# Where the stores of the first 63 rows stand in the queues, and how the last two row groups are cut into pieces

## The chip, the cores and the metric

The kernel runs on one core of one Trainium2 chip. The metric is the device time of one execution in microseconds (us), as the median of several runs. The profile is of one execution more, and times inside it are counted from the start of its span.

## What is computed

```python
N, D = (8192, 64)                      # x: 8192x64, adj: 8192x8192, u: 8192x64, all float32
keep = (u >= 0.1).astype(x.dtype)
x_drop = x * keep / (1.0 - 0.1)
y = x + jnp.matmul(adj, x_drop)        # adj has few nonzeros but is stored dense: 268 MB
m = jnp.mean(y, axis=-1, keepdims=True)
v = jnp.var(y, axis=-1, keepdims=True)
return (y - m) / jnp.sqrt(v + 1e-5)
```

The host part of the kernel reorders adj into blocks, so that every transfer reads one contiguous stretch of memory. Nothing is computed there.

## The kernel before, in words

The 8192 rows of the output are 64 rows on each of the 128 partitions (`KT` = 64). A "row" below is one of these 64, so 128 rows of the output. For each row, the products run over 64 tiles of adj with 128x128 elements (64 KB each), one for each value of t. The weights are the 64 columns of x_drop for t, the moving operand is the adj tile, and even and odd t go to the lower and the upper half of the partitions of the accumulator (line 203). The result is transposed and in two halves. A copy of it to `acc_sb` (line 253, `take`) and a product with `twofold`, a stacked identity matrix (line 210, `turn_back`), turn it back and add the halves. VectorE then adds x, takes mean and variance of each row and normalises it (`normalise`, lines 256 to 288), with ScalarE's square root in between (line 178). The normalised rows overwrite x in SBUF (`normed` is `x_nat`).

Rows come in groups. Twelve groups of 5 rows (`FULL`, `R`) run in loops; their adj comes in three slots of 24, 24 and 16 tiles into a ring that holds exactly one group. Then follow two small groups that are written out: 3 rows (rows 60 to 62), and the last row (63). `TAIL` lists the pieces in which their adj is loaded, in tiles. In the 3-row group a tile is three 128x128 blocks wide (192 KB), and in the last row it is one (64 KB). In the text, T0.0 to T0.4 are the pieces of the 3-row group and T1.0, T1.1, ... those of the last row.

Queues and their order:

- SyncE (SP) issues x and u and all of adj in one queue (q1 in the profile). Before each load it waits until TensorE has used the part of the ring that the load overwrites (lines 154 and 160).
- ScalarE (ACT) issues the three stores in a second queue (q10). The store of the first 60 rows (line 186, 1920 KB) goes out when the twelfth group is normalised, the store of rows 60 to 62 (line 191, 96 KB) when the 3-row group is, and that of the last row (line 196, 32 KB) at the end. Then ACT waits until all three have landed.
- TensorE (PE) takes the pieces in order (lines 227 to 246). After the first piece of the last row it turns back the 3-row group and adds x of the last row to `final` (line 241).
- The last three tiles of the last row (`DIRECT` = 2 pieces) are multiplied the other way round, straight into `final` (line 235), so that the copy of the accumulator and its product with `twofold` (line 246) run before the last tile is there.
- VectorE ends with the statistics of `final`, the reciprocal and the normalisation (lines 310 to 316).

Of the kernel before, what the change touches and what calls it, by code (L numbers as in the profile page):

```python
# [6 lines left out]
D = 64  # L7
P = 128
KT = N // P
# [6 lines left out]
R = 5  # L16
FULL = 12
TILE = R * P
# [3 lines left out]
MAIN = FULL * SLOTS  # L22
# [3 lines left out]
COLS = TILE // 2  # L26
SPLIT = TILE // COLS

TAIL = [(3, [26, 15, 11, 8, 4]), (1, [13, 16, 12, 8, 6, 4, 2, 2, 1])]
LAST = len(TAIL) - 1  # L30
FIRST_ROW = [FULL * R + sum(rows for rows, _ in TAIL[:n]) for n in range(len(TAIL))]
FIRST_PIECE = [sum(len(tiles) for _, tiles in TAIL[:n]) for n in range(len(TAIL))]

DIRECT = 2
HALVED = KT - sum(TAIL[LAST][1][-DIRECT:])
X_PARTS = 4
PART = KT * D // X_PARTS
PT = KT // X_PARTS

assert FULL * R + sum(rows for rows, _ in TAIL) == KT  # L40
assert all(sum(tiles) == KT for _, tiles in TAIL) and sum(SLOT_TILES) == KT

# [12 lines left out]
def build(nc: bass.Bass, xu: bass.AP, adj: bass.AP, out: bass.AP):  # L55
# [6 lines left out]
    out_rows = out.rearrange("(p t) d -> p (t d)", p=P)  # L62
# [6 lines left out]
    def tail_block(start, width):  # L69
        first = (FULL * RING + start) * P  # L70
        return adj[first:first + width * P].rearrange("(p c) -> p c", p=P)

    with ExitStack() as ctx:
        def sb(name, shape):
            return ctx.enter_context(nc.sbuf_tensor(name, shape, fp32))

        def sem(name):
            return ctx.enter_context(nc.semaphore(name))

        def ps(name, cols):  # L80
            return ctx.enter_context(nc.psum_tensor(name, [P, cols], fp32))

        adj_ring = sb("adj_ring", [P, RING])
# [4 lines left out]
        x_drop = x_and_u[:, KT * D:2 * KT * D]  # L88

        normed = x_nat  # L90
        identity = sb("identity", [P, P])
        twofold = sb("twofold", [P, D])
        eps = sb("eps", [P, 1])
        acc_sb = sb("acc_sb", [P, TILE])
# [12 lines left out]
        acc = [ps(f"acc{b}", 512) for b in range(SPLIT)]  # L107
        tail_acc = [ps(f"tail_acc{n}", 512) for n in range(len(TAIL))]
        back = ps("back", 512)
        final = ps("final", 512)  # L110
# [6 lines left out]
        adj_used = sem("adj_used")  # L117
# [2 lines left out]
        zeros_ready = sem("zeros_ready")  # L120
        identity_ready = sem("identity_ready")
        twofold_ready = sem("twofold_ready")
        halved_ready = sem("halved_ready")
        acc_copied = sem("acc_copied")
        back_ready = sem("back_ready")
        sum_ready = sem("sum_ready")
# [6 lines left out]
        std_ready = sem("std_ready")  # L133
        rstd_ready = sem("rstd_ready")
        normed_ready = sem("normed_ready")
        final_stats = sem("final_stats")
        final_var = sem("final_var")
        out_stored = sem("out_stored")
# [4 lines left out]
        def _(sp):  # L143
# [12 lines left out]
            for n in range(len(TAIL)):  # L156
                for i, (_, _, at, width) in enumerate(pieces(n)):
# [2 lines left out]
                    sp.wait_ge(adj_used, MAIN - SLOTS + slot)  # L160
                    sp.dma_start(adj_ring[:, at:at + width], tail_block(at, width)).then_inc(piece_loaded[n][i], 16)  # L161

        @block.gpsimd
        def _(pool):
            nc.gpsimd.memset(eps[:], EPS).then_inc(eps_ready, 1)  # L165
            nc.gpsimd.memset(identity[:], 0.0).then_inc(zeros_ready, 1)
            pool.wait_ge(zeros_ready, 1)
            nc.gpsimd.affine_select(out=identity[:], in_=identity[:], compare_op=ALU.not_equal, fill=1.0,
                                    base=0, pattern=[[-1, P]], channel_multiplier=1).then_inc(identity_ready, 1)

            pool.wait_ge(identity_ready, 1)
            nc.gpsimd.tensor_tensor(twofold[:], identity[:, 0:D], identity[:, D:P], ALU.add).then_inc(twofold_ready, 1)

        @block.scalar
        def _(act):
            def root(n, rows):
                act.wait_ge(squares_ready, n + 1)
                nc.scalar.activation(std[:, 0:rows], squares[:, 0:rows], ACT.Sqrt, scale=1.0 / D,  # L178
                                     bias=eps[:]).then_inc(std_ready, 1)

            act.wait_ge(eps_ready, 1)
            with act.Fori(0, FULL) as g:
                root(g, R)
            act.wait_ge(normed_ready, FULL)
            cols = slice(0, FULL * R * D)
            act.dma_start(out_rows[:, cols], normed[:, cols]).then_inc(out_stored, 16)
            for n in range(LAST):
                root(FULL + n, TAIL[n][0])
            act.wait_ge(normed_ready, FULL + LAST)
            cols = slice(FULL * R * D, (KT - 1) * D)  # L190
            act.dma_start(out_rows[:, cols], normed[:, cols]).then_inc(out_stored, 16)
            act.wait_ge(final_var, 1)
            nc.scalar.activation(std[:, 0:1], mean_var[:, 1:2], ACT.Sqrt, bias=eps[:]).then_inc(std_ready, 1)  # L193
            act.wait_ge(normed_ready, FULL + LAST + 1)
            cols = slice((KT - 1) * D, KT * D)
            act.dma_start(out_rows[:, cols], normed[:, cols]).then_inc(out_stored, 16)
            act.wait_ge(out_stored, 16 * 3)

        @block.tensor
        def _(pe):  # L200
            def product(into, cols, at, t, end):
                h = t % 2
                return nc.tensor.matmul(into[h * D:(h + 1) * D, 0:cols], x_drop[:, t * D:(t + 1) * D],  # L203
                                        adj_ring[:, at:at + cols], start=(t < 2), stop=(t >= end - 2))

            def turn_back(rows, done):

                pe.wait_ge(acc_copied, done + 1)
                for r in range(rows):
                    last = nc.tensor.matmul(back[:, r * D:(r + 1) * D], acc_sb[:, r * P:(r + 1) * P], twofold[:],  # L210
                                            start=True, stop=True)
                last.then_inc(back_ready, 1)

            pe.wait_ge(twofold_ready, 1)
            with pe.Fori(0, FULL) as g:
                for s in range(SLOTS):
                    pe.wait_ge(chunk_loaded[s], (g + 1) * 16)
                    for pair in range(SLOT_FIRST[s], SLOT_FIRST[s] + SLOT_TILES[s], 2):
                        if pair % PT == 0:
                            pe.wait_ge(drop_ready, pair // PT + 1)  # L220
                        for b in range(SPLIT):
                            for t in (pair, pair + 1):
                                last = product(acc[b], COLS, t * TILE + b * COLS, t, KT)
                    last.then_inc(adj_used, 1)
                turn_back(R, g)

            for n, (rows, _) in enumerate(TAIL):
                for i, (before, count, at, _) in enumerate(pieces(n)):
                    pe.wait_ge(piece_loaded[n][i], 16)
                    for t in range(before, before + count):  # L230
                        col = at + (t - before) * rows * P
                        if n < LAST or t < HALVED:
                            last = product(tail_acc[n], rows * P, col, t, KT if n < LAST else HALVED)
                        else:
                            last = nc.tensor.matmul(final[:, 0:D], adj_ring[:, col:col + P],  # L235
                                                    x_drop[:, t * D:(t + 1) * D], start=False, stop=(t == KT - 1))
                    last.then_inc(adj_used, 1)
                    if n == LAST and i == 0:

                        turn_back(TAIL[n - 1][0], FULL + n - 1)  # L240
                        nc.tensor.matmul(final[:, 0:D], identity[:], x_nat[:, (KT - 1) * D:KT * D],  # L241
                                         start=True, stop=False)
                    if n == LAST and i == len(TAIL[n][1]) - 2:

                        pe.wait_ge(acc_copied, FULL + LAST + 1)
                        nc.tensor.matmul(final[:, 0:D], acc_sb[:, 0:P], twofold[:], start=False, stop=False)  # L246

        @block.vector
        def _(dve):
            def take(into, cols, used):  # L250
                dve.wait_ge(adj_used, used)
                for b, part in enumerate(into):
                    last = nc.vector.tensor_copy(acc_sb[:, b * cols:(b + 1) * cols], part[:, 0:cols])  # L253
                last.then_inc(acc_copied, 1)
# [36 lines left out]
            for i in range(X_PARTS):  # L291
                cols = slice(i * PART, (i + 1) * PART)
# [9 lines left out]
            for n in range(LAST):  # L302
                rows = TAIL[n][0]
                take([tail_acc[n]], rows * P, MAIN + FIRST_PIECE[n] + len(TAIL[n][1]))
                normalise(FULL + n, FIRST_ROW[n], rows)

            take([tail_acc[LAST]], P, MAIN + FIRST_PIECE[LAST] + len(TAIL[LAST][1]) - DIRECT)

            dve.wait_ge(adj_used, MAIN + FIRST_PIECE[LAST] + len(TAIL[LAST][1]))
            nc.vector.bn_stats(stats[:, 0, :], final[:, 0:D]).then_inc(final_stats, 1)  # L310
            dve.wait_ge(final_stats, 1)
            nc.vector.bn_aggr(mean_var[:], stats[:, 0, :]).then_inc(final_var, 1)  # L312
# [38 lines left out]
```

## Time and profile before

| | us |
|---|---|
| median of 3 runs (lowest, highest) | 645.89 (645.62, 645.92) |
| the profiled execution | 645.73 |
| its span, first to last instruction | 643.8 |
| PE busy | 512.4 (80%) |
| DVE busy | 60.8 (9%) |
| ACT busy | 19.6 (3%) |
| data moved | 274.80 MB, mean 427 GB/s |

The strip of the 16 DMA engines shows 9 (90% or more) in every one of its 40 slices but the last. PE idles 114.1 us in the main loop, always for adj. In the page, busy time of PE is modelled, since matmuls overlap; PEld is its weight load. "DMA to landing" is the time from the issue of a transfer to the arrival of its semaphore. MB and GB count 1000s, KB in the list of DMA issues counts 1024s.

### The profile page before, as it was taken

To read this page: it belongs to the slowest core of one execution; us is meant where nothing else is said; L and a number is where in the kernel's file an instruction comes from. 1 tells how busy PE (TensorE), PEld (TensorE's weight loads), DVE (VectorE), ACT (ScalarE), POOL (GpSimd) and SP (SyncE) were. 2 spreads that over 40 slices of the span, in tenths; PEclk is the share of its full clock that TensorE was granted. 3 is DMA by queue.
4 is the path that set the end of the run, shared out by engine and by line. 5 is a ranking of instruction groups with operands and counts; after the bars stand their busy time and mean duration, and the time that the engine had idled before them with its cause. 6 is when DMAs were issued, how large, how long until landed. Compare 5 with 4: busy or idle time off the path is not lost.

```text
span 643.8 us, 7619 instructions
## 1 busy us (share of the span) xinstructions
PE 512.4 (80%) x3458; PEld 265.4 (41%) x3458; DVE 60.8 (9%) x268; ACT 19.6 (3%) x26; POOL 1.1 (0%) x8
## 2 busy tenths in 40 slices
PE   0088798698798698798698798798798887888987
PEld 0044344344344344444344444444443443444436
DVE  1200200200200200100200200200200110110202
ACT  0000000000000000000000000000000000000000
POOL 0000000000000000000000000000000000000000
PEclk9997988988988987989878988988987987979999
DMA  9999999999999999999999999999999999999996
GB/s 383 428 429 444 432 428 440 428 435 440 428 431 444 428 428 448 428 428 448 428 428 448 428 428 448 428 428 448 428 428 448 428 428 448 428 428 408 421 427 253
DMA packets 7780, 274.80 MB, mean 427 GB/s; under 512 B 992, under 2 KB 1504, under 8 KB 2272
## 3 DMA queue, kind: packets, MB, share of 16 engines
q1 hardware_dynamic: 7344, 272.63, 98.2%
q10 hardware_dynamic: 432, 2.10, 0.8%
q8 instruction: 4, 0.07, 0.0%
HBM read 272.63 MB, written 2.10 MB: 427 GB/s over the span
## 4 chain that ended last, share of the span: by engine, by line
DMA 69%; PE 30%; SPq 0%; issue 0%; DVE 0%; ACT 0%
DMA adj_ring<-adj_blocks 69%; PE acc L203 28%; PE tail_acc L203 2%; SPq L146 0%; PE final L235 0%; PE back L210 0%; SPq L161 0%; SPq L148 0%; DVE x_and_u L316 0%; PE final L246 0%; ACT std L193 0%; DVE stats L310 0%; PE final L241 0%; DVE mean_var L312 0%; DVE rstd L314 0%
## 5 line engine op out<-in xcount | busy, mean ns | idle before, releaser
L203 PE MATMUL acc<-adj_ring,x_and_u 128*64 128x320 f32 x3072 | 465.4, 468 | 114.1 <-DMA adj_ring<-adj_blocks 114.1
L203 PEld LDWEIGHTS acc<-adj_ring,x_and_u 128*64 128x64 f32 x3072 | 233.2, 149 | 341.0 <-DMA adj_ring<-adj_blocks 122.3
L253 DVE COPY acc_sb<-acc 128x320 f32<-128x320 f32 x24 | 10.7, 486 | 517.4 <-PE acc L203 517.4
L203 PE MATMUL tail_acc<-adj_ring,x_and_u 128*64 128x384 f32 (+1 forms) x250 | 29.0, 384 | 2.2 <-DMA adj_ring<-adj_blocks 2.1
L210 PE MATMUL back<-twofold,acc_sb 128*128 128x64 f32 x126 | 16.8, 280 | 11.9 <-DVE acc_sb L253 11.9
L210 PEld LDWEIGHTS back<-twofold,acc_sb 128*128 128x128 f32 x126 | 15.0, 191 | 18.8 <-DVE acc_sb L253 18.7
L178 ACT ACTIVATE std<-squares,eps 128x5 f32<-128x5 f32 (+1 forms) x13 | 3.9, 300 | 615.1 <-DVE squares L278 615.1
L203 PEld LDWEIGHTS tail_acc<-adj_ring,x_and_u 128*64 128x64 f32 x250 | 15.9, 137 | 14.9 <-issue 10.8
L178 ACT ACT_TABLE_LOAD x12 | 15.4, 1283 | 1.2 <-POOL eps L165 1.0
L284 DVE TENSOR_SCALAR x_and_u<-summed,mean,rstd 128x64 f32 (+1 forms) x63 | 15.2, 309 | 0.5
L262 DVE BATCH_NORM_STATS2 stats<-summed 128x6 f32<-128x64 f32 x63 | 9.3, 213 | 0.4
L258 DVE TENSOR_TENSOR summed<-back,x_and_u 128x320 f32<-128x320 f32 (+1 forms) x13 | 6.3, 482 | 20.3 <-PE back L210 20.3
L293 DVE SCALAR_TENSOR_TENSOR x_and_u<-x_and_u 128x1024 f32<-128x1024 f32 x4 | 4.9, 1220 | 12.9 <-DMA x_and_u<-xu 12.9
L253 DVE COPY acc_sb<-tail_acc 128x384 f32<-128x384 f32 (+1 forms) x2 | 0.9, 426 | 23.1 <-PE tail_acc L203 23.1
L281 DVE RECIPROCAL rstd<-std 128x5 f32<-128x5 f32 (+1 forms) x13 | 2.5, 190 | 4.8 <-ACT std L178 4.8
L297 DVE TENSOR_SCALAR x_and_u<-x_and_u 128x1024 f32<-128x1024 f32 x4 | 2.8, 693 | 0.1
L276 DVE TENSOR_SCALAR mean<-twice_mean 128x5 f32<-128x5 f32 (+1 forms) x13 | 2.2, 172 | 0.0
L268 DVE TENSOR_TENSOR gap<-stats 128x5 f32<-128x5 f32 (+1 forms) x13 | 2.2, 169 | 0.5
L269 DVE TENSOR_TENSOR within<-stats 128x5 f32<-128x5 f32 (+1 forms) x13 | 2.1, 160 | 0.0
L270 DVE TENSOR_TENSOR twice_mean<-stats 128x5 f32<-128x5 f32 (+1 forms) x13 | 2.1, 160 | 0.0
L278 DVE TENSOR_TENSOR squares<-within,between 128x5 f32<-128x5 f32 (+1 forms) x13 | 2.1, 160 | 0.0
L272 DVE SCALAR_TENSOR_TENSOR between<-gap 128x5 f32<-128x5 f32 (+1 forms) x13 | 2.0, 157 | 0.0
(19 smaller groups left out, 5.8 us busy)
## 6 DMA issues: line engine op xcount, KB each, us to landing
adj_ring<-adj_blocks SPq DMA_DIRECT2D x24, 7680.0 KB, 33.3
adj_ring<-adj_blocks SPq DMA_DIRECT2D x12, 5120.0 KB, 36.9
adj_ring<-adj_blocks SPq DMA_DIRECT2D x1, 4992.0 KB, 26.0
x_and_u<-xu SPq DMA_DIRECT2D x1, 4096.0 KB, 12.1
adj_ring<-adj_blocks SPq DMA_DIRECT2D x1, 2880.0 KB, 17.6
adj_ring<-adj_blocks SPq DMA_DIRECT2D x1, 2112.0 KB, 26.2
out<-x_and_u ACTq DMA_DIRECT2D x1, 1920.0 KB, 13.8
adj_ring<-adj_blocks SPq DMA_DIRECT2D x1, 1536.0 KB, 29.9
```

Source lines behind the costliest of these rows:

```text
L178: nc.scalar.activation(std[:, 0:rows], squares[:, 0:rows], ACT.Sqrt, scale=1.0 / D, bias=eps[:]).then_inc(std_ready, 1)
L203: return nc.tensor.matmul(into[h * D:(h + 1) * D, 0:cols], x_drop[:, t * D:(t + 1) * D], adj_ring[:, at:at + cols], start=(t < 2), stop=(t ...
L210: last = nc.tensor.matmul(back[:, r * D:(r + 1) * D], acc_sb[:, r * P:(r + 1) * P], twofold[:], start=True, stop=True)
L253: last = nc.vector.tensor_copy(acc_sb[:, b * cols:(b + 1) * cols], part[:, 0:cols])
L258: nc.vector.tensor_tensor(summed[:, 0:rows * D], back[:, 0:rows * D], x_nat[:, bass.ds(row * D, rows * D)], ALU.add).then_inc(sum_ready, 1)
L262: last = nc.vector.bn_stats(stats[:, r, :], summed[:, r * D:(r + 1) * D])
L268: nc.vector.tensor_tensor(gap[:, 0:rows], m0, m1, ALU.subtract).then_inc(gap_ready, 1)
L276: nc.vector.tensor_scalar(mean[:, 0:rows], twice_mean[:, 0:rows], 0.5, None, ALU.mult)
L281: nc.vector.reciprocal(rstd[:, 0:rows], std[:, 0:rows]).then_inc(rstd_ready, 1)
L284: last = nc.vector.tensor_scalar(normed[:, bass.ds((row + r) * D, D)], summed[:, r * D:(r + 1) * D], mean[:, r:r + 1], rstd[:, r:r + 1], A ...
L293: nc.vector.scalar_tensor_tensor(out=x_drop[:, cols], in0=x_drop[:, cols], scalar=P_DROP, in1=x_nat[:, cols], op0=ALU.is_ge, op1=ALU.mult) ...
L297: nc.vector.tensor_scalar(x_drop[:, cols], x_drop[:, cols], 1.0 / (1.0 - P_DROP), None, ALU.mult).then_inc(drop_ready, 1)
```

## The change

The stores of the first 60 rows and of rows 60 to 62 are no longer issued by ScalarE in q10 but by SyncE in q1, behind the last piece of adj. Each waits there for the same semaphore as before. The store of the last row stays with ScalarE. The pieces of the 3-row group become 24, 16, 10, 8 and 6 tiles (they were 26, 15, 11, 8 and 4), and those of the last row 20, 18, 14, 8 and 4 (they were 13, 16, 12, 8, 6, 4, 2, 2 and 1). All 64 tiles of the last row go through the transposed accumulator, so that its copy and the product with `twofold` come after the last tile. That product now raises a semaphore, `final_ready`, on which VectorE waits.

```diff
-TAIL = [(3, [26, 15, 11, 8, 4]), (1, [13, 16, 12, 8, 6, 4, 2, 2, 1])]
+TAIL = [(3, [24, 16, 10, 8, 6]), (1, [20, 18, 14, 8, 4])]
...
-DIRECT = 2
-HALVED = KT - sum(TAIL[LAST][1][-DIRECT:])
...
                     sp.dma_start(adj_ring[:, at:at + width], tail_block(at, width)).then_inc(piece_loaded[n][i], 16)
+
+            sp.wait_ge(normed_ready, FULL)
+            cols = slice(0, FULL * R * D)
+            sp.dma_start(out_rows[:, cols], normed[:, cols]).then_inc(out_stored, 16)
+            sp.wait_ge(normed_ready, FULL + LAST)
+            cols = slice(FULL * R * D, (KT - 1) * D)
+            sp.dma_start(out_rows[:, cols], normed[:, cols]).then_inc(out_stored, 16)
...
             with act.Fori(0, FULL) as g:
                 root(g, R)
-            act.wait_ge(normed_ready, FULL)
-            cols = slice(0, FULL * R * D)
-            act.dma_start(out_rows[:, cols], normed[:, cols]).then_inc(out_stored, 16)
             for n in range(LAST):
                 root(FULL + n, TAIL[n][0])
-            act.wait_ge(normed_ready, FULL + LAST)
-            cols = slice(FULL * R * D, (KT - 1) * D)
-            act.dma_start(out_rows[:, cols], normed[:, cols]).then_inc(out_stored, 16)
...
-                        if n < LAST or t < HALVED:
-                            last = product(tail_acc[n], rows * P, col, t, KT if n < LAST else HALVED)
-                        else:
-                            last = nc.tensor.matmul(final[:, 0:D], adj_ring[:, col:col + P],
-                                                    x_drop[:, t * D:(t + 1) * D], start=False, stop=(t == KT - 1))
+                        last = product(tail_acc[n], rows * P, col, t)
...
-                    if n == LAST and i == len(TAIL[n][1]) - 2:
-
-                        pe.wait_ge(acc_copied, FULL + LAST + 1)
-                        nc.tensor.matmul(final[:, 0:D], acc_sb[:, 0:P], twofold[:], start=False, stop=False)
+            pe.wait_ge(acc_copied, FULL + LAST + 1)
+            nc.tensor.matmul(final[:, 0:D], acc_sb[:, 0:P], twofold[:], start=False, stop=True).then_inc(final_ready, 1)
...
-            take([tail_acc[LAST]], P, MAIN + FIRST_PIECE[LAST] + len(TAIL[LAST][1]) - DIRECT)
-
-            dve.wait_ge(adj_used, MAIN + FIRST_PIECE[LAST] + len(TAIL[LAST][1]))
+            take([tail_acc[LAST]], P, MAIN + FIRST_PIECE[LAST] + len(TAIL[LAST][1]))
+            dve.wait_ge(final_ready, 1)
```

## Rows read from the trace of the kernel before

**Rows 1.** Page, part 3: the stores' queue, packets, MB, share of 16 engines.

```profile
q10 hardware_dynamic: 432, 2.10, 0.8%
```

**Rows 2.** Busy time of each engine by stretch; last columns PEclk, DMA share, GB/s.

```profile
583.30:605.00 21.70, 21.70 (x160) 11.37 (x160) 0.00 (x0) 0.00 (x0) 0.00 (x0) 1.00 0.99 429
611.00:625.00 14.00, 11.94 (x74) 5.05 (x72) 0.19 (x1) 0.00 (x0) 0.00 (x0) 1.00 0.97 414
637.00:638.00 1.00, 1.00 (x22) 1.00 (x20) 0.00 (x0) 0.00 (x0) 0.00 (x0) 1.00 0.60 194
638.00:639.00 1.00, 1.00 (x24) 1.00 (x22) 0.00 (x0) 0.00 (x0) 0.00 (x0) 1.00 0.24 70
```

**Rows 3.** Chain that ended last, in order of time: start us, us, what.

```profile
627.28 5.67 PE tail_acc L203 x50
...
633.99 5.39 PE tail_acc L203 x96
```

**Rows 4.** Timeline of PE's weight loads: start us, us, what, [idle before <-releaser].

```profile
606.01 1.19 PEld L210 LDWEIGHTS back<-twofold,acc_sb 128*128 128x128 f32 x10 [1.55 <-DVE acc_sb L253]
...
607.65 0.14 PEld L203 LDWEIGHTS tail_acc<-adj_ring,x_and_u 128*64 128x64 f32 x2 [0.18 <-issue]
...
620.22 0.14 PEld L203 LDWEIGHTS tail_acc<-adj_ring,x_and_u 128*64 128x64 f32 x1 [0.19 <-issue]
623.08 0.20 PEld L203 LDWEIGHTS tail_acc<-adj_ring,x_and_u 128*64 128x64 f32 x4 [2.72 <-DMA adj_ring<-adj_blocks]
...
631.21 0.85 PEld L203 LDWEIGHTS tail_acc<-adj_ring,x_and_u 128*64 128x64 f32 x16 [0.50 <-DMA adj_ring<-adj_blocks]
```

**Rows 5.** Page, part 6: DMA issues, count, KB each, us from issue to landing.

```profile
out<-x_and_u ACTq DMA_DIRECT2D x1, 1920.0 KB, 13.8
...
adj_ring<-adj_blocks SPq DMA_DIRECT2D x1, 832.0 KB, 32.9
adj_ring<-adj_blocks SPq DMA_DIRECT2D x1, 512.0 KB, 31.8
...
out<-x_and_u ACTq DMA_DIRECT2D x1, 96.0 KB, 2.9
adj_ring<-adj_blocks SPq DMA_DIRECT2D x1, 64.0 KB, 13.7
out<-x_and_u ACTq DMA_DIRECT2D x1, 32.0 KB, 1.5
```

**Rows 6.** Timeline of SP's queue: issues of T1.0, T1.3 and T1.8.

```profile
598.26 0.43 SPq L161 DMA_DIRECT2D adj_ring<-adj_blocks  x1
...
605.06 0.33 SPq L161 DMA_DIRECT2D adj_ring<-adj_blocks  x1
...
625.61 1.68 SPq L161 DMA_DIRECT2D adj_ring<-adj_blocks  x1
```

**Rows 7.** Timeline of all engines, from the first store's issue to the last's.

```profile
611.22 0.38 ACTq L186 DMA_DIRECT2D out<-x_and_u  x1
...
631.42 0.56 DVE L253 COPY acc_sb<-tail_acc 128x384 f32<-128x384 f32 x1 [20.23 <-PE tail_acc L203]
...
632.88 0.88 PE L210 MATMUL back<-twofold,acc_sb 128*128 128x64 f32 x6
...
633.92 5.46 PE L203 MATMUL tail_acc<-adj_ring,x_and_u 128*64 128x128 f32 x96
...
636.65 0.34 ACTq L191 DMA_DIRECT2D out<-x_and_u  x1
...
639.50 0.29 DVE L253 COPY acc_sb<-tail_acc 128x128 f32<-128x128 f32 x1 [2.88 <-PE tail_acc L203]
639.85 0.43 PE L246 MATMUL final<-twofold,acc_sb 128*128 128x64 f32 x2
...
640.54 0.23 DVE L310 BATCH_NORM_STATS2 stats<-final 128x6 f32<-128x64 f32 x1 [0.75 <-PE final L235]
...
641.93 0.34 ACTq L196 DMA_DIRECT2D out<-x_and_u  x1
```

More of the change, by code:

```diff
@@ L122, in build @@
         twofold_ready = sem("twofold_ready")
-        halved_ready = sem("halved_ready")
         acc_copied = sem("acc_copied")
@@ L135, in build @@
         normed_ready = sem("normed_ready")
+        final_ready = sem("final_ready")
         final_stats = sem("final_stats")
@@ L200, in _, with product @@
         def _(pe):
-            def product(into, cols, at, t, end):
+            def product(into, cols, at, t):
                 h = t % 2
                 return nc.tensor.matmul(into[h * D:(h + 1) * D, 0:cols], x_drop[:, t * D:(t + 1) * D],
-                                        adj_ring[:, at:at + cols], start=(t < 2), stop=(t >= end - 2))
+                                        adj_ring[:, at:at + cols], start=(t < 2), stop=(t >= KT - 2))
             def turn_back(rows, done):
@@ L222, in _ @@
                             for t in (pair, pair + 1):
-                                last = product(acc[b], COLS, t * TILE + b * COLS, t, KT)
+                                last = product(acc[b], COLS, t * TILE + b * COLS, t)
                     last.then_inc(adj_used, 1)
```

## Prediction, made before the changed kernel was run

> **What bounds the kernel now.** I read the strips of the page first, then the busy time by stretch, then PE's weight loads and the landings of the pieces over the last 40 us. The strip of the DMA engines is full to the last slice, and in a stretch with loads alone they move 429 GB/s at a share of 0.99 [rows 2]. So the time is that of the bytes, plus what comes after the last byte of adj, plus whatever else stands in the queue before that byte. The stores do stand there: q10 moves 2.10 MB [rows 1], of which 1.97 MB (1920 KB) go out at 611.22, while adj is still being loaded [rows 5, 7].
>
> The last 40 us need a closer look, because there the bound changes hands. From 606.01 on PE works off the turning back of the twelfth group and then the pieces of the 3-row group [rows 4]. It keeps up a pace of one 3-row tile per (620.22 - 607.65) / 39 = 0.322 us, while a tile of 192 KB (0.197 MB) takes the DMA engines 0.197 / 0.429 = 0.458 us. PE has a stock, though: T0.0 and T0.1 are there when it starts on them. It runs without a wait for 41 tiles. Then its weight loads stand 2.72 us until T0.2 has landed (623.08), waits again before T0.3, and once more, 0.50 us, before T1.0 at 631.21 [rows 4]. The chain that ended last shows the rest as PE alone: from 627.28 to the end of the products at 639.38, in two long blocks [rows 3]. So the end of this kernel is set by both: the pieces land only just ahead of PE. Landings are issue plus time to landing [rows 5, 6]: T1.0 at 598.26 + 32.9 = 631.2, T1.3 at 605.06 + 31.8 = 636.9, T1.8 at 625.61 + 13.7 = 639.3.
>
> **Stores behind the loads.** While the store of 1920 KB was in flight (611.22 to 625.0) all queues together moved 414 GB/s, a little under the 429 of loads alone [rows 2]. So the loads lost what the store took. Without it, each piece that lands after 625 lands 1.966 / 0.427 = 4.6 us earlier (by 0.414 it would be 4.75; I take the smaller). The store of 96 KB is worth 0.2 us, of the last tiles only.
>
> The wait that moves to SP costs nothing: behind it in SP's queue stand only the two stores. The first one's condition is met at 611.2, the second one's as long after the 3-row group is turned back as before, 636.65 - (632.88 + 0.88) = 2.9 us [rows 7], which is 634.2 by the times below, while the first store is still running. Their price is the time after the loads. The DMA engines do the same bytes in all, in another order, and none of them idles before the end, so q1 should run dry when the loads and stores of before did. The load share ends around 637.3 (0.60 in 637 to 638), with a few slow engines on until 639.0 (0.24) [rows 2], and the store of 96 KB landed at 636.65 + 2.9 = 639.55 [rows 5, 7]. I take 639.6 for the two moved stores. Loads alone then end around 637.3 - 4.6 = 632.7, with stragglers to 634.7.
>
> No row shows a store running with no load beside it. Its cost is bounded from below by the joint rate (4.6 us for 1.966 MB, the row for which the engines were 97% busy), and from above by its own pace beside the loads, 13.8 us [rows 5]. I take 4.6, because the joint rate hardly fell while it ran: it looks like sharing, and not like a limit of the store.
>
> The Trainium skill (DMA: Bandwidth & Descriptors, Specifications) gives a core about 358 GB/s of HBM. The loads here run at 429 [rows 2], so the trace does not agree for reads; for writes alone no row shows it. By that figure the two stores would take 5.8 us where I have 4.8, and would land an estimated 1 us later, at 640.6.
>
> **New pieces of the 3-row group.** The same 64 tiles. T0.0 (24 tiles, 2 fewer) lands before 607.2, but PE is not free sooner: its weight loads for turning back end at 606.01 + 1.19 = 607.20 [rows 4]. So PE starts where it did. Is it then ever short of data? 40 tiles keep it busy to about 620.2. T0.2 (50 tiles) lands about 618.2: the 41st tile was there at 614.05, and 9 more take 4.1 us. T0.4 lands about 624.6 (T1.0's landing below, less 20 small tiles of 0.0655 MB / 0.427 = 0.153 us each), and PE wants it after 58 tiles, at 626.0. So PE runs through, and 24 tiles after 620.22 it starts T1.0, at 620.22 + 24 x 0.322 = **627.96**, where it was 631.21. That is 3.25 us. PE is now the bound: the other 1.4 us of the 4.6 are not on its path.
>
> T1.0 must be there by then. It has 20 tiles now. 13 landed at 631.2 and 49 (through T1.3) at 636.9, 0.158 us a tile, so 20 would have at 632.3, and 4.6 earlier that is 627.7. The margin is only 0.3 us, and this is the weakest link of the sum. If it fails, the rest shifts by what is missing.
>
> **New pieces of the last row.** Before, the products up to the turning back took 632.88 - 631.21 = 1.67 us for 13 tiles, and 48 tiles took 5.46, or 0.114 each [rows 4, 7]. Seven more before the turning back: it starts at 627.96 + 1.67 + 0.80 = 630.43. The copy that it needs (0.56 us, right after the last 3-row product [rows 7]) has 2.4 us of cover. Turning back and adding x take 633.92 - 632.88 = 1.04: 631.47. Then 44 tiles at 0.114 take 5.01: the products end at **636.48**, against 639.38. The pieces land by the same reckoning (interpolated, less 4.6) at 630.5 (T1.1, wanted 631.5), 632.8 (T1.2, 633.5), 634.1 (T1.3, 635.1) and 634.7 (T1.4, 636.0), each 0.7 to 1.3 us ahead. Four transfers fewer save nothing on the path. A piece fewer means a coarser wait, which costs nothing as long as PE is behind the data.
>
> **Last row without direct products.** Three tiles move from one form to the other at the same price (they are in the 44). Copy and product with `twofold` came beside the direct products, and now stand alone on the path. The copy starts 0.12 us after the last product, as before (639.38 to 639.50), takes 0.29, then 0.06, then 0.43 for the product [rows 7]. VectorE's statistics start at 636.48 + 0.12 + 0.29 + 0.06 + 0.43 + 0.02 = 637.40, against 640.54 [rows 7]. So this way of ending takes 0.92 us from the last transposed product to the statistics, where the old took 1.16 with its three direct tiles.
>
> **Sum.** Everything after that is unchanged: the last store is issued at 641.93 - 3.14 = 638.79 and lands 1.5 us later, at 640.3, against 643.4. The moved stores (639.6) have landed by then, with 0.7 us to spare. Span 643.8 - 3.14 = 640.66, and the profiled execution 645.73 - 3.14 = 642.6. The median of the runs lies 0.16 above the profiled execution, so I forecast **642.7**.
>
> **Rivals.**
>
> *Data still last* (PE waits at T1.0 or later). For it: the margin of 0.3 us, and slow engines that finish up to 2 us behind the mean, which decide when a piece counts as landed. Against: removing the store takes the same off every engine. If the pieces come 0.3 to 1 us later than I reckon, the time is 643.0 to 643.5. Chance 0.13.
>
> *Stores last, but not badly.* The two stores run at some 300 GB/s with nothing beside them: 6.9 us instead of 4.8, landing at 641.7 instead of 640.3 for the last row's, span 642.1, time 644.1. For it: reading SBUF and writing HBM with all engines is not in the trace. At 358 GB/s it would be 642.9 to 643.0. Chance 0.09.
>
> *Stores last, and slower than before.* The 13.8 us were the store's own limit, 1.966 MB at 142 GB/s, and not its share. It would then start at 632.7 and land at 646.5: span 646.9, time 648.8, 2.9 us slower. It decides from a length of 643.4 - 632.7 = 10.7 us, or 184 GB/s. Against it: beside the store the total would then have had room to be the full 429 and was 414, and the loads gave way to it. Chance 0.06.
>
> *The stores do not wait behind the loads.* If SP's queue let the store's packets in among the loads, the landings would be as before, PE's gaps would stay, and the end would differ only by the shape of the last row: 645.5 to 646.2. Against: pieces of one queue landed in the order of their issue. Chance 0.05. I count here too whatever gives back the gain without my seeing it.
>
> **How the numbers follow.** The forecast (642.3 to 643.0) has 0.67, the four rivals 0.13, 0.09, 0.06 and 0.05. Range for 8 in 10: from 642.1 (the forecast, less a spread like that of the three runs) to 644.0, which takes in late pieces and most of the milder stores. A measurement of this kernel can tell about 0.2%, 1.3 us, from no change. So faster means under 644.6: 0.67 + 0.13 + 0.09 and a little of the rest, less something for an unseen loss, 0.87. Same 0.06, slower 0.07.
>
> **What would show it.** In the profile of the changed kernel: weight loads of PE from 607.3 to about 630 with no wait for adj_ring in them; T1.0's first near 628.0; the statistics of `final` near 637.4; the last store issued near 638.8; and the stores from SP landing by 640. A wait of PE for adj_ring before T1.0 would mean that the data is still last. A share of the DMA engines near 1 but well under 420 GB/s after 633, or a last landing from SP's queue after 640.5, would mean that the stores are. If T1.0 is taken up at 631 as before, the stores were not behind the loads, and the whole sum is wrong.

## The result, and the profile after

The changed kernel takes 644.43 us (median) against 645.75 for the kernel before, in runs of the same session: a ratio of 0.998, with a 95% interval of 0.9973 to 0.9986. So it is faster by about 0.2%, where 0.5% was forecast (642.7 us), and the time lies above the range (642.1 to 644.0). What no part of the prediction speaks of is the spread. The executions of before all lie within 0.6 us (645.53 to 646.14). Those of the changed kernel fall into three groups: 2 at 642.4 and 642.5, 10 between 643.9 and 644.6, and 7 between 645.2 and 645.6. The twentieth, in a slow state of the chip, took 868.78 us at a mean granted clock of 0.57, and says nothing about the change.

The profiled execution took 644.05 us with a span of 642.2: 1.7 less than before, and 1.5 more than forecast. Busy time by stretch, of the changed kernel (last columns PEclk, DMA share, GB/s), as in [rows 2]:

```profile
583.30:605.00 21.70, 21.70 (x150) 11.40 (x152) 0.00 (x0) 0.00 (x0) 0.00 (x0) 0.92 0.99 427
611.00:625.00 14.00, 14.00 (x90) 6.24 (x88) 1.47 (x8) 0.30 (x1) 0.00 (x0) 1.00 1.00 419
...
637.00:638.00 1.00, 0.99 (x20) 0.75 (x14) 0.00 (x0) 0.00 (x0) 0.00 (x0) 1.00 0.33 121
638.00:639.00 1.00, 0.43 (x2) 0.30 (x2) 0.36 (x2) 0.00 (x0) 0.00 (x0) 1.00 0.17 55
```

The first line is the one to look at. PE is busy for the whole stretch in both kernels, but with a granted clock of 0.92 here and 1.00 in [rows 2], and its matmul records are 150 instead of 160. Slices of 1 us show where that is:

```profile
583.00:584.00 1.00, 0.73 (x6) 0.48 (x8) 0.00 (x0) 0.00 (x0) 0.00 (x0) 1.00 0.66 287
584.00:585.00 1.00, 1.00 (x10) 0.53 (x6) 0.00 (x0) 0.00 (x0) 0.00 (x0) 0.81 0.85 369
585.00:586.00 1.00, 1.00 (x6) 0.48 (x4) 0.00 (x0) 0.00 (x0) 0.00 (x0) 0.50 1.52 655
586.00:587.00 1.00, 1.00 (x6) 0.42 (x5) 0.00 (x0) 0.00 (x0) 0.00 (x0) 0.50 0.38 164
587.00:588.00 1.00, 1.00 (x8) 0.42 (x6) 0.00 (x0) 0.00 (x0) 0.00 (x0) 0.50 1.14 492
588.00:589.00 1.00, 1.00 (x10) 0.54 (x8) 0.00 (x0) 0.00 (x0) 0.00 (x0) 0.99 1.52 655
```

For some 3.4 us, from about 584.6 on, the clock is at 0.50 (1.2 instead of 2.4 GHz). PE has then been at work again for 1.3 us, after a wait of 2.13 us. Over this stretch the changed kernel (first line) has 16 matmul records where the kernel before (second line) has 28, while the transfers are the same in both:

```profile
584.60:588.00 3.40, 3.40 (x16) 1.57 (x14) 0.00 (x0) 0.00 (x0) 0.00 (x0) 0.50 0.89 386
584.60:588.00 3.40, 3.40 (x28) 1.83 (x26) 0.00 (x0) 0.00 (x0) 0.00 (x0) 1.00 0.89 386
```

The timeline of PE shows what that does to the last 5-row group, and what came before it:

```profile
565.12 16.01 PE L201 MATMUL acc<-adj_ring,x_and_u 128*64 128x320 f32 x96 [3.54 <-DMA adj_ring<-adj_blocks]
583.26 23.44 PE L201 MATMUL acc<-adj_ring,x_and_u 128*64 128x320 f32 x160 [2.13 <-DMA adj_ring<-adj_blocks]
607.70 1.33 PE L208 MATMUL back<-twofold,acc_sb 128*128 128x64 f32 x10 [0.99 <-DVE acc_sb L245]
```

The same view of the kernel before has the second and third lines as:

```profile
583.27 21.75 PE L203 MATMUL acc<-adj_ring,x_and_u 128*64 128x320 f32 x160 [2.10 <-DMA adj_ring<-adj_blocks]
606.01 1.33 PE L210 MATMUL back<-twofold,acc_sb 128*128 128x64 f32 x10 [0.99 <-DVE acc_sb L253]
```

The block of the last two slots starts at the same moment and takes 23.44 us instead of 21.75. Everything behind it is 1.69 us late. The chain that ended last is PE from there to the end (start us, us, what), where [rows 3] begins only at 627.28:

```profile
594.87 11.87 PE acc L201 x88
...
607.70 1.33 PE back L208 x10
609.03 22.97 PE tail_acc L201 x168
632.00 0.81 PE back L208 x6
632.81 0.22 PE final L235 x2
633.04 4.98 PE tail_acc L201 x88
...
638.11 0.30 DVE acc_sb L245
...
638.46 0.45 PE final L238 x2
...
638.93 0.24 DVE stats L301
```

No wait for adj_ring stands in it. The stores, from the page's list of issues and from the timeline (they answer to [rows 5, 7]):

```profile
out<-x_and_u SPq DMA_DIRECT2D x1, 1920.0 KB, 24.8
...
out<-x_and_u SPq DMA_DIRECT2D x1, 96.0 KB, 3.7
out<-x_and_u ACTq DMA_DIRECT2D x1, 32.0 KB, 1.5
```

```profile
612.90 0.34 SPq L162 DMA_DIRECT2D out<-x_and_u  x1
...
635.70 0.34 SPq L165 DMA_DIRECT2D out<-x_and_u  x1
...
640.31 0.37 ACTq L194 DMA_DIRECT2D out<-x_and_u  x1
```

Issue plus time to landing puts them at 637.7 (612.90 + 24.8), 639.4 (635.70 + 3.7) and 641.8 (640.31 + 1.5), so the last row's store is the last.

### The profile page after: what moved, and what is told of

The parts are those of the page before. It is cut to its first block, busy times and chain, and to the rows that moved or that the text cites. A ratio compares the mean times of both kernels' runs of the same rounds, so it can differ in the third digit from the quotient of the medians.

```text
span 642.2 us, 7615 instructions
## 1 busy us (share of the span) xinstructions
PE 511.6 (80%) x3458; PEld 264.7 (41%) x3458; DVE 60.7 (9%) x268; ACT 19.6 (3%) x26; POOL 1.1 (0%) x8
## 4 chain that ended last, share of the span: by engine, by line
DMA 64%; PE 34%; DVE 0%; issue 0%; SPq 0%; ACT 0%; DVEq 0%
DMA adj_ring<-adj_blocks 64%; PE acc L201 29%; PE tail_acc L201 4%; PE back L208 0%; DVE acc_sb L245 0%; SPq L143 0%; PE final L238 0%; SPq L145 0%; DVE x_and_u L307 0%; ACT std L191 0%; DVE stats L301 0%; PE final L235 0%; DVE mean_var L303 0%; DVE rstd L305 0%; DVEq L243 0%
## 6 DMA issues: line engine op xcount, KB each, us to landing
out<-x_and_u SPq DMA_DIRECT2D x1, 1920.0 KB, 24.8
```

## The experiments

**Theory A:** after the change PE sets the end from the second slot of the last 5-row group on (583.3), with no wait for data behind that. What PE loses to a granted clock of 0.50 there stands in the time, and it differs from execution to execution. Before, PE waited for T0.2, T0.3 and T1.0 [rows 4], and these waits took up the loss. **Theory B:** the spread comes from the transfers, whose landings vary with the stores behind them.

### The stores alone

```diff
 # the kernel before, with
+            sp.wait_ge(normed_ready, FULL)              # the two stores behind the last piece, in SP's queue
+            ...
-            act.wait_ge(normed_ready, FULL)             # and gone from ScalarE
-            ...
```

> The kernel before with only the two stores moved to SyncE's queue behind the last piece; pieces and direct products as before. Theory A (the end is set by PE from the last 5-row group on, so half-clock stretches of PE there show in the time): PE starts the last row near 628.0, statistics of final near 637.3 where no such stretch falls, so 642.5 at best, and otherwise that plus 1.7 us for each half-clock stretch: single executions spread over 642.4 to 645.5, median about 644. Theory B (the transfers' landings vary): here nine small pieces instead of five stand in front of the stores, so the spread should be other than that of the changed kernel, and PE should show waits for adj_ring.

Measured: 644.24 us (643.87 to 645.35, 10 executions), ratio 0.9979 (0.997 to 0.9988). That is the changed kernel's time within the spread of both, so the stores are what moved it. Its profiled execution is one of the late ones, 645.32 us:

```profile
583.30:589.30 6.00, 5.94 (x24) 2.72 (x26) 0.00 (x0) 0.00 (x0) 0.00 (x0) 0.51 1.01 437
589.30:605.00 15.70, 15.70 (x120) 8.22 (x118) 0.00 (x0) 0.00 (x0) 0.00 (x0) 1.00 0.97 418
```

```profile
583.36 24.62 PE L204 MATMUL acc<-adj_ring,x_and_u 128*64 128x320 f32 x160 [3.30 <-DMA adj_ring<-adj_blocks]
...
610.23 22.38 PE L204 MATMUL tail_acc<-adj_ring,x_and_u 128*64 128x384 f32 x154
```

Here the half-clock stretch lasts for the first 6 us of the block, which takes 24.62 us: 2.87 more than 21.75. 645.32 - 2.87 = 642.45, the fastest group. The 3-row products run on without a wait. None of its 10 executions was as fast as that group, which the expectation had allowed for.

### The pieces and the ending alone

```diff
 # the changed kernel, with
-            sp.wait_ge(normed_ready, FULL)              # the two stores gone from SP's queue
-            ...
+            act.wait_ge(normed_ready, FULL)             # and back in ScalarE's, as before
+            ...
```

> The changed kernel with the two stores back in ScalarE's queue. Theory A: the store takes 4.6 us from the loads again, T1.0 (20 tiles) lands near 632.3, PE waits for it, and the end comes at 632.3 + 2.25 + 1.04 + 5.0 + 0.92 = 641.5 for the statistics of final, against 640.54 before: 646.7, and nearly the same in all executions (within 0.6 us), since PE waits for data after any half-clock stretch of the last 5-row group. Theory B: the spread of 3 us stays, since the pieces are those of the changed kernel.

Measured: 646.90 us (646.62 to 647.03, 10 executions), ratio 1.0017 (1.0008 to 1.0026). The spread is gone with the stores, and the time came where the interpolation of landings put it. The profile (646.78 us) has a half-clock stretch too, and waits for data behind it:

```profile
583.32 23.21 PE L200 MATMUL acc<-adj_ring,x_and_u 128*64 128x320 f32 x160 [3.02 <-DMA adj_ring<-adj_blocks]
...
626.49 4.94 PE L200 MATMUL tail_acc<-adj_ring,x_and_u 128*64 128x384 f32 x28 [1.35 <-DMA adj_ring<-adj_blocks]
632.36 2.40 PE L200 MATMUL tail_acc<-adj_ring,x_and_u 128*64 128x128 f32 x40 [0.93 <-DMA adj_ring<-adj_blocks]
```

1.5 us were lost in the block (23.21 - 21.75), and PE waits for data behind it, so they do not set the time. The chain of this profile goes through T1.0, from its issue to its landing (start us, us):

```profile
599.28 33.02 DMA adj_ring<-adj_blocks
```

T1.0, now 20 tiles, lands at 632.3, as expected, where the 13 tiles of before landed at 631.2. That is 1.1 us, about what this kernel is slower by; the piece and the new ending were not changed one at a time.

### The changed kernel again

> The changed kernel itself, for its spread on this chip and another profile. Theory A: executions in groups near 642.4, 644.1 and 645.4; the profile shows in its last 60 us as much PE time at half clock as its time is over 642.4 (1.7 us for each 3.4 us at half clock in which PE was busy). Theory B: the profile shows a late landing, and no clock below 1.00 after 583.

Measured: 644.15 us (642.53 to 645.23, 9 executions: one at 642.5, five at 643.9 to 644.2, three at 645.1 to 645.2), ratio 0.9976 (0.9966 to 0.9986). The profiled one, 644.15 us, has its half-clock stretch in the same place, a block of 23.45 us, and PE turns back the twelfth group at 607.69.

### PE's idle time filled

```diff
+            def dummy(count):
+                for _ in range(count):
+                    nc.tensor.matmul(final[0:D, 0:512], twofold[:], x_drop[:, 0:512], start=True, stop=True)
+
+            pe.wait_ge(drop_ready, 1)
             with pe.Fori(0, FULL) as g:
+                dummy(12)
                 for s in range(SLOTS):
...
                     last.then_inc(adj_used, 1)
+                    if s == 0:
+                        dummy(9)
```

> The changed kernel with idle time of PE in the main loop filled by products that nobody reads (12 of 512 columns before the wait for the first slot, 9 before that for the second, about 5 and 4 us at full clock). Theory A: the granted clock stays 1.00 in the last groups, PE starts the 3-row group at 607.3 or a little before, and all executions lie at 642.3 to 642.9. Theory B: the time spreads over 642.4 to 645.6 as before.

Measured: 717.01 us, ratio 1.1107 (1.1092 to 1.1122). A miss, by a size of my own: one of these products takes 0.85 us and not 0.43, so they overran the idle time and made PE the bound of the main loop. The clock did stay at 1.00 (mean 0.998). With 6 and 5 of them in place of 12 and 9:

> The changed kernel with PE's idle time in the main loop filled less than in the first try: 6 products of 512 columns before the wait for the first slot and 5 before that for the second, 0.85 us each by the first try's trace, so 5.1 and 4.3 us out of 6.8 and 5.4 that are idle when PE runs at full clock. Theory A (PE sets the end, and half-clock stretches after the wait for the second slot of the last 5-row group make the spread): no granted clock under 1.00 after the first groups, the block of products that starts near 583.3 takes 21.7 us, all executions at 642.3 to 642.9. Theory B (landings vary): the spread of 3 us stays.

Measured: **642.51 us** (642.31 to 642.64, 5 executions), ratio 0.995 (0.9935 to 0.9964). The spread of 3 us is gone, and the time is the fastest group's. PE does more work than in the changed kernel, and the kernel is 1.6 to 1.9 us faster (644.15 and 644.43 in its two rounds of runs). The profile (642.31 us):

```profile
583.21 21.75 PE L201 MATMUL acc<-adj_ring,x_and_u 128*64 128x320 f32 x160 [0.71 <-DMA adj_ring<-adj_blocks]
605.96 1.33 PE L208 MATMUL back<-twofold,acc_sb 128*128 128x64 f32 x10 [0.99 <-DVE acc_sb L253]
607.21 23.04 PE L201 MATMUL tail_acc<-adj_ring,x_and_u 128*64 128x384 f32 x168
630.19 0.88 PE L208 MATMUL back<-twofold,acc_sb 128*128 128x64 f32 x6
```

The granted clock is 1.00 over 583.3 to 640. The stores, the pieces and their queues are those of the changed kernel, so this run speaks against Theory B by itself. T1.0's weight loads begin a little late here:

```profile
627.70 1.43 PEld L201 LDWEIGHTS tail_acc<-adj_ring,x_and_u 128*64 128x64 f32 x23 [0.30 <-DMA adj_ring<-adj_blocks]
```

Between other pairs of weight loads the pause is 0.18 us [rows 4], so T1.0 landed about 0.1 us after PE could have used it.

### Only the idle time before the second slot, or only that before the first

In the first variant `dummy(2)` stands behind slot 0 and nothing before it; in the second, `dummy(6)` stands before slot 0 and nothing behind it.

> The changed kernel with PE's idle time filled only before the wait for the second slot (2 products of 512 columns, 1.7 us of some 2.1 to 3.3). Theory A, in its narrow form: it is the idle time right before the second slot of the last 5-row group that brings the half-clock stretch which costs time. Then the block that starts near 583.3 takes 21.7 us and all executions lie at 642.3 to 642.9, although the clock still falls after each wait for the first slot (mean granted clock near 0.93 to 0.95). If the stretches come from anything else, the spread stays.

Measured: 642.51 us (642.34 to 642.52, 5 executions), ratio 0.9949 (0.9936 to 0.9963). The clock still falls elsewhere (mean 0.928), which costs nothing. So filling the idle time right before the second slot is enough. It was filled in all twelve groups, and not tried in the last one only.

> The changed kernel with PE's idle time filled only before the wait for the first slot (6 products). The first slot then runs at full clock and is done near 578, 3 us sooner, so PE idles 5.2 us before the second slot instead of 2 to 3. Theory A: the half-clock stretch after it comes in every execution and costs at least as much as in the changed kernel: 643.7 to 645.7, none near 642.4, median about 645. A theory by which more PE work in the loop simply keeps the whole kernel at full clock would have 642.5.

Measured: 644.06 us (642.37 to 645.89, 7 executions), ratio 0.9975 (0.9961 to 0.999). The spread stays, as Theory A has it, and more PE work alone does not remove it. But the expectation that none would be near 642.4 was wrong: three are at 642.4 to 642.7. The profiled one (642.72 us) is among these, and its line shows a longer wait than the changed kernel's, with no loss behind it:

```profile
583.61 21.75 PE L201 MATMUL acc<-adj_ring,x_and_u 128*64 128x320 f32 x160 [3.44 <-DMA adj_ring<-adj_blocks]
```

The test is less clean than it was meant to be. The six products overran the idle time, from 561.89 to 567.09, while the first slot was there at about 565.1 (565.12 in the changed kernel's timeline). So the first slot ran at full clock but was done at 580.17 and not near 578, and PE idled 3.44 us and not 5.2. Two of the seven executions, 644.72 and 645.89, lie outside the three groups.

The length of the wait does not by itself decide whether the clock falls. The kernel before, too, had 2.10 us of it without a fall and the changed kernel 2.13 with one.

### More PE work ahead of the 3-row group

```diff
+            for _ in range(2):
+                nc.tensor.matmul(final[0:D, 0:512], twofold[:], x_drop[:, 0:512], start=True, stop=True)
             for n, (rows, _) in enumerate(TAIL):
```

> The kernel before with 2 products that nobody reads (1.7 us of PE) between the turning back of the last 5-row group and the 3-row group. Theory A: they go where PE waits for T0.2, T0.3 and T1.0, and the time is 645.7 to 646.0, unchanged. If PE were on the path here already from 606 on, it would be 647.4.

Measured, on the kernel before: 645.83 us (645.59 to 646.91, 10 executions, nine of them under 646.1), ratio 1.0002 (0.9993 to 1.0012). Its profile (645.73 us) has a half-clock stretch besides, so that 3.4 us more of PE time were absorbed (the 3-row products begin at 610.72, and at 607.27 in the kernel before):

```profile
583.26 23.44 PE L203 MATMUL acc<-adj_ring,x_and_u 128*64 128x320 f32 x160 [2.53 <-DMA adj_ring<-adj_blocks]
...
610.72 22.33 PE L203 MATMUL tail_acc<-adj_ring,x_and_u 128*64 128x384 f32 x152
```

PE turns back the twelfth group at 607.69 instead of 606.01 [rows 4], has 1.7 us more to do, and then runs through the 3-row group, since the data is now there. The two products stand behind the block, so the half-clock stretch is one of the kernel before, and it does not show in the time.

> warm_less with the same 1.7 us of PE work ahead of the 3-row group. Theory A: nothing absorbs it, so 1.7 us more than warm_less: 644.2, in a narrow band. If data is as late as PE there, less than 1.7 us is added to it or the same 1.7 is absorbed in part (the data's margin is 0.3 us at T1.0).

Measured, on the changed kernel with its idle time filled: 644.13 us (644.05 to 644.7, 9 executions), which is 1.62 more than `warm_less`. In the trace the two products hold the 3-row group up by 1.8 us. The same work is free in the one kernel and paid nearly in full in the other.

### What the stores and the pieces are worth now

> warm_less without the two moved stores: the first 63 rows of the output are not written, only the last is. This prices the stores where they now stand. If they are hidden behind the last row's products and its end, as forecast, 642.4 to 642.6, unchanged. If they still cost something (their bytes, or a delay of the last store), up to 1 us less.

Measured: 642.54 us (642.46 to 642.56, 4 executions). This kernel leaves the first 63 rows of the output unwritten. Without the two moved stores the time is the same: they are hidden.

> The kernel before with the stores moved and PE's idle time filled as in warm_less, but with its own 14 pieces and the direct products. By the sum of the prediction the new pieces and the new ending gain nothing on the path once the stores are gone: statistics of final at 640.54 - 3.25 = 637.3, so 642.3 to 642.7, as warm_less. If fewer pieces matter, this is up to 1 us slower.

Measured: 642.39 us (642.27 to 642.55, 4 executions), ratio 0.9948 (0.9933 to 0.9963). With the 14 old pieces and the direct products the kernel is no slower, so the new pieces and the new ending gain nothing.

### Four slots

```diff
-SLOT_TILES = [24, 24, 16]
+SLOT_TILES = [20, 18, 14, 12]
...
-TAIL = [(3, [24, 16, 10, 8, 6]), (1, [20, 18, 14, 8, 4])]
+TAIL = [(3, [12, 14, 14, 10, 8, 6]), (1, [10, 18, 16, 12, 8])]
```

> The changed kernel with the 5-row groups in four slots (20, 18, 14, 12 tiles) instead of three (24, 24, 16), the 3-row group in 12, 14, 14, 10, 8, 6 tiles and the last row in 10, 18, 16, 12, 8. PE is then done with the last 5-row group some 3 us sooner after its data. Theory A: PE waits for data again in the last two groups, so half-clock stretches are absorbed; products end near 635.4, the stores from SyncE's queue are among the last to land (639.4), 641.7 to 642.3, with a spread under 1 us. Theory B: spread of 3 us stays, since there are the same stores in the same place.

Measured: 643.10 us (643.05 to 643.19, 5 executions), ratio 0.9958 (0.9944 to 0.9972). The spread falls to 0.14 us, and PE waits for data again behind the 5-row groups:

```profile
605.34 8.61 PE L201 MATMUL tail_acc<-adj_ring,x_and_u 128*64 128x384 f32 x52
614.72 8.04 PE L201 MATMUL tail_acc<-adj_ring,x_and_u 128*64 128x384 f32 x48 [0.77 <-DMA adj_ring<-adj_blocks]
623.00 6.03 PE L201 MATMUL tail_acc<-adj_ring,x_and_u 128*64 128x384 f32 x48 [0.23 <-DMA adj_ring<-adj_blocks]
```

That these waits are what narrows the spread is not shown: in this profile the clock is 1.00 from 572 to 640 and there was no loss to absorb. The expectation missed the time by 0.8 us. The last landing on the chain is that of T1.2, at 632.59, and the products end at 636.94 instead of 635.4:

```profile
596.42 36.17 DMA adj_ring<-adj_blocks
632.64 4.30 PE tail_acc L201 x72
```

The DMA engines finish about 1 us later than in the changed kernel (0.77 busy in 637 to 638, where that has 0.33). Whether its 13 more loads are the reason was not tried.

Theory B is out. In `warm_less` the same stores and pieces stand in the same places, and all five executions agree; in `four_slots` the stores do too. The landing of T1.0 does not move with the time either: 627.8 (599.46 + 28.3) in the profile of the changed kernel, in which PE lost 1.7 us, and 627.6 (597.67 + 29.9) in that of `warm_less`, in which it lost nothing.

## Why the prediction was wrong

**The step that failed** is the first sentence of the part on the 3-row group: "So PE starts where it did." It fixed PE's start by the end of its own turning back, at 607.20, and took that from one execution in which the clock was 1.00 from 583 on. The reading of the rows was right, and the use of it was not. From 583.3 on PE had become the bound, and the length of its block is not a constant. It is 21.75 us at full clock, and was 23.44 (`after`), 23.45 (`after_same`), 24.62 (`stores_only`), 23.21 (`pieces_only`) and 23.44 (`before_pad`) in five other profiled executions. The term missing from the sum is this loss: 0, 1.5 to 1.7, or 2.9 us in these profiles. The profiled execution of the changed kernel pays 1.7, and so much lies between the forecast 642.7 and the median, 644.4. None of the rivals had it. They all asked what the transfers would do.

The sign of it stood in front of me. The page's strip of the granted clock dips in every group of the main loop, and the wait before the second slot (2.10 us in the last group) is in the trace of before. I had costed the time as the critical path of one execution, and the kernel before hides the loss so well that its 20 executions spread by 0.6 us only. The Trainium skill (TensorE: Matmul & The Clock Gate, Part 1) says that the clock follows how busy the engine has been recently, and that the number of slow matmuls at a kernel's start differs from run to run. The traces agree with the first: with the idle time before the block filled, none of the 18 executions of `warm_less`, `fill_second`, `warm_no_stores` and `warm_old_pieces` lies above 642.64 us. They show the second in the middle of a kernel too, with 0 to 2.9 us lost in one and the same place.

**The rest of the sum held**, where the clock did not fall. `warm_less` measured 642.51 and `fill_second` 642.51, against 642.6 for the profiled execution and 642.7 for the median.

- Stores behind the loads: right. They were to land at 639.6 and landed at 639.4 in the profile of the changed kernel. `warm_no_stores` shows them hidden. The store is not limited to the 142 GB/s at which it went beside the loads: it landed at 637.7, where that rival has 646.5.
- By the Trainium skill's 358 GB/s of HBM for a core (DMA: Bandwidth & Descriptors, Specifications) they would have landed at an estimated 640.6. They landed 1.2 us sooner, and from 635 to 637, behind the last landing of adj (634.6), 400 GB/s were moved. So the trace does not agree with it for stores either.
- PE through the 3-row group without a wait: right, in all profiles with the stores moved and three slots. The weakest link, T1.0, landed where it was reckoned (627.6 to 627.8, forecast 627.7), but the margin of 0.3 us was not there: PE at full clock is earlier than forecast, and its weight loads wait about 0.1 us for T1.0 in `warm_less`. The changed kernel, 1.7 us late, did not test it. In `warm_less` the turning back begins at 630.19, against a forecast of 630.43.
- New pieces and ending: 0.92 us from the last product to the statistics was the forecast; the chain gives 638.01 (633.04 + 4.98, rounded) to 638.93, which is 0.92. Together they gain nothing (`warm_old_pieces`), and alone, with the stores in front of the data, they cost 1.2 us (`pieces_only`).

**The bound after the change** was named correctly: "PE is now the bound: the other 1.4 us of the 4.6 are not on its path." The conclusion that was missed is the next one: whatever varies on PE now shows. The range was made from bounds on the transfers, and its upper end, 644.0, had no room for a loss of PE.

## What to carry to other kernels

When a change hands the bound from one engine to another, look at what the new bound does over the whole stretch for which it now has no slack, and not only at the end. Check in particular whether its clock, in other groups of the same trace, falls after waits like the one that starts this stretch; a narrow spread of the old kernel says nothing about it, since the slack hid it. Here a few products that nobody reads, put where TensorE waits, are worth 1.6 to 1.9 us of 644, and those before the wait for the second slot were enough.

## What the runs showed that was not expected

- The granted clock falls in some executions and not in others after waits of 2.1 to 3.4 us. The loss is 0, 1.5 to 1.7 or 2.9 us in the profiles, and most executions lie in three groups to match, but not all (644.72 and 645.89 in `fill_first`). What decides was not settled.
- Products with 512 columns into one half of the partitions took 0.43 us for each of their two instructions, at a granted clock of 1.00, while the kernel's own, with 320 columns into alternate halves, took 0.136 us each (21.75 us for 160). That is nearly twice as long per column. That two products on different halves overlap would explain it, but was not tried by itself.
- Stores with nothing beside them go nearly as fast as loads. In the changed kernel's profile the last piece of adj landed at 634.6 (607.6 + 27.0), and in the two slices from 635 to 637 the engines moved (399 + 400) / 2 = 400 GB/s at a share of 0.96, against 429 at 0.99 for loads alone [rows 2].
